# Values, convolution, u and head projections in blocks of 512 tokens instead of whole channel groups

## The reference, cut to what matters

```
xn   = x * rsqrt(mean(x*x) + 1e-6) * rms_w          # after a layernorm
V    = xn @ Wv.T + bv                                # 512 channels
vc   = causal depthwise convolution of V, 4 taps     # per channel, over the tokens
u    = silu(vc + conv_b)
dyn, seldt, selB, selC, beta, r_gate, u_gate = u @ (small matrices).T   # together 11 x 32 = 352 columns
...                                                  # coefficients of each head from these, 32 heads
scan over the tokens with k = K * sel_B, v = u * gate, read out with q = Q(u) * sel_C
...                                                  # group norm, gate, output projection, router, experts
```

## Time and profile before

| what | value |
|---|---|
| median of 3 runs | 1971.14 us (1969.77 to 1975.34) |
| the profiled execution's own time | 1970.1 us |
| its span | 1968.0 us |
| PE busy | 1347.6 us (68%) |
| DVE busy | 1436.4 us (73%) |
| ACT busy | 331.1 us (17%) |
| mean granted TensorE clock | 0.821 |

### The profile page before, as it was taken

The page is one execution under the profiler, slowest core; times in us unless marked ns, Lnnn a source line. Parts: engine busy times, 40 slices in busy tenths (PEclk is TensorE's granted clock), DMA queues, the critical chain, the costliest instruction groups (busy, mean ns, idle before and its releaser), DMA issues.

```text
span 1968.0 us, 12778 instructions
## 1 busy us (share of the span) xinstructions
PE 1347.6 (68%) x4176; PEld 753.7 (38%) x4176; DVE 1436.4 (73%) x2382; ACT 331.1 (17%) x592; POOL 0.2 (0%) x4
## 2 busy tenths in 40 slices
PE   2690276753088869356559999948388877399994
PEld 1250022212044445223335555535154445166662
DVE  3718799997899988856385999978999989500003
ACT  2312000001000002142332111122000011223331
POOL 0000000000000000000000000000000000000000
PEclk9895566665599989668879999969699989599997
DMA  3000010101011120210011222112111010122221
GB/s 123 0 0 0 11 43 32 43 11 64 0 32 43 43 85 11 86 49 0 0 32 57 94 72 88 54 64 86 43 43 53 22 43 0 48 66 82 75 78 43
DMA packets 49955, 89.66 MB, mean 46 GB/s; under 512 B 4450, under 2 KB 39650, under 8 KB 48867
## 3 DMA queue, kind: packets, MB, share of 16 engines
q1 hardware_dynamic: 49890, 88.87, 13.1%
HBM read 68.93 MB, written 19.92 MB: 45 GB/s over the span
## 4 chain that ended last, share of the span: by engine, by line
DVE 50%; PE 35%; issue 9%; ACT 4%; SPq 1%; DMA 1%; DVEq 0%; ACTq 0%
PE ps L513 9%; PE ps L525 9%; PE ps L389 5%; PE ps L364 4%; DVE work L1009 4%; DVE uT L719 3%; PE ps L390 3%; DVE small L988 3%; DVE work L989 2%; DVE small L724 2%; DVE work L1048 2%; DVE work L1035 2%; DVE kz L1018 2%; DVE work L959 2%; DVE work L719 2%
## 5 line engine op out<-in xcount | busy, mean ns | idle before, releaser
L440 PE MATMUL ps<-wshare,uT 128*128 128x512 f32 x512 | 251.0, 647 | 53.6 <-DVE kz L1018 53.6
L525 PE MATMUL ps<-kz 128*128 128x256 f32 x1024 | 243.5, 381 | 46.1 <-ACT kz L679 46.1
L389 PE MATMUL ps<-wshare,xnT 128*128 128x512 f32 x256 | 166.1, 783 | 142.4 <-DVE wshare L905 142.4
L513 PE MATMUL ps<-kz 128*128 128x512 f32 x512 | 246.7, 605 | 7.9 <-DMA kz<-in_w 7.2
L525 PEld LDWEIGHTS ps<-kz 128*128 128x128 f32 x1024 | 195.5, 191 | 127.2 <-issue 59.1
L440 PEld LDWEIGHTS ps<-wshare,uT 128*128 128x128 f32 x512 | 103.9, 209 | 181.0 <-issue 121.8
L1148 DVE TENSOR_TENSOR kz<-kz,b_s 128x256 f32<-128x256 f32 x32 | 13.6, 425 | 212.7 <-ACT kz L663 211.8
L679 ACT ACTIVATE kz<-ps,small 128x512 f32<-128x512 f32 x128 | 87.8, 687 | 396.2 <-PE ps L513 396.2
L389 PEld LDWEIGHTS ps<-wshare,xnT 128*128 128x128 f32 x256 | 55.4, 240 | 221.2 <-DVE wshare L905 146.3
L513 PEld LDWEIGHTS ps<-kz 128*128 128x128 f32 x512 | 97.7, 194 | 91.3 <-issue 84.4
L364 PE MATMUL ps<-wshare,uT 128*128 128x352 f32 x256 | 79.9, 476 | 37.5 <-ACT uT L598 37.5
(11 more groups left out here) (223 smaller groups left out, 1836.6 us busy)
## 6 DMA issues: line engine op xcount, KB each, us to landing
kz<-in_w SPq DMA_DIRECT2D x128, 256.0 KB, 3.0
kap_d<-kz SPq DMA_DIRECT2D x26, 512.0 KB, 2.8
kz<-kap_d SPq DMA_DIRECT2D x26, 512.0 KB, 3.3
uT<-in_x SPq DMA_DIRECT2D x2, 2048.0 KB, 8.0
wshare<-in_wq SPq DMA_DIRECT2D x2, 2048.0 KB, 7.9
coef<-in_x SPq DMA_DIRECT2D x2, 2048.0 KB, 7.8
wshare<-in_wk SPq DMA_DIRECT2D x2, 1024.0 KB, 12.1
x_d<-coef SPq DMA_DIRECT2D x1, 2048.0 KB, 6.2
```

The costliest lines, as they stand in the source:

```text
L389: mm(o, xnT[:, k, j * P:(j + 1) * P], wk_s[:, k, c, :], start=(k == 0), stop=False)
L440: t = mm(ps[:, 2 * (j % 2) + c, :], uT3[:, k, j * P:(j + 1) * P], wq_s[:, k, c, :], start=(k == 0), stop=(k == KI - 1))
L513: t = mm(ps[:, 4 + i % 2, :], w1_r[r][:, k, (f % 2) * P:(f % 2 + 1) * P], x2T[:, k, n * 512:(n + 1) * 512], start=(k == 0), stop=(k == KM ...
L525: t = mm(ps[:, 6 + q // 2, (q % 2) * DM:(q % 2 + 1) * DM], hbuf(i)[:, q * P:(q + 1) * P], w2_r[r][:, f % 2, :], start=(f == 0 and q % 2 == ...
```

## The change

It does five things:

- PE makes the values by blocks of tokens, in the order 3, 0, 1, 2, with the four groups inside a block.
- There are four `vbuf` buffers, one for each group: three in `work` and one in `kz`. The third reaches over the place of the rope table. ACT evicts all 16 units first, and then applies Silu to 16 pieces of 128 x 512, in the order of the blocks 0 to 3.
- DVE does the convolution by blocks. In a block it interleaves the four groups, so that each instruction waits for one four places earlier, and not for the one in front (`mark` and `after` in place of `link`). From block 1 on, it evicts the four head tiles of the block before, once a block is done.
- The head projections wait for u block by block, not for all of it. DVE no longer waits for each eviction to end before the next.
- The rope table is loaded after the convolution in both batches, since its place is in use until then. In batch 1 this stands behind the loads of the first four pairs of expert weights and before the others.

```diff
@@ -90,7 +90,9 @@
         w2_r = [kz[:, 9728 + 1024 * r:10240 + 1024 * r].rearrange("p (f n) -> p f n", f=2) for r in range(WR)]
         r_tok = kz[:, 13312:17408].rearrange("p (j d) -> p j d", j=L)
         VB = 19 * P
-        vbuf = [work[:, i * VB:(i + 1) * VB].rearrange("p (j c) -> p j c", c=P) for i in range(2)]
+        vbuf = [v.rearrange("p (j c) -> p j c", c=P) for v in
+                (work[:, 0:VB], work[:, VB:2 * VB], work[:, 2 * VB:3 * VB], kz[:, 0:VB])]
+        NORD = (3, 0, 1, 2)
         sall = coef[:].rearrange("p (q j h) -> p q j h", q=NSM, j=L)
         sall_j = coef[:].rearrange("p (q j h) -> p j q h", q=NSM, j=L)
         uT3 = uT[:].rearrange("p (g t) -> p g t", g=KI)
@@ -241,8 +243,7 @@
                 sp.dma_start(wk_s, wk.rearrange("(k p) i n -> p k i n", p=P)).then_inc(wk_loaded, 16)
 
             def load_rope(b):
-                if b > 0:
-                    sp.wait_ge(kq_used, b * 2 * L)
+                sp.wait_ge(conv_done, b * NV + NV)
                 sp.dma_start(HS(14), rope[:]).then_inc(rope_loaded, 16)
 
             def choose_experts(b):
@@ -281,16 +282,17 @@
             load(wo_s[:], wo.rearrange("(k p) n -> p k n", p=P))
             load(wr_s[:], wr.rearrange("(k p) n -> p k n", p=P))
             load(group[:], group_d[:])
-            load_rope(0)
             for b in range(B):
                 if b > 0:
                     load_wa(b)
-                    load_rope(b)
                     load_x(b)
                     sp.wait_ge(x1_ready, b * L)
                     sp.dma_start(x1_d[:], x1_tok).then_inc(x1_stored, 16)
                     chosen = choose_experts(b - 1)
-                    load_pairs(b - 1, chosen, 0, pairs_for(UNITS[0]))
+                    load_pairs(b - 1, chosen, 0, WR)
+                load_rope(b)
+                if b > 0:
+                    load_pairs(b - 1, chosen, WR, pairs_for(UNITS[0]))
 
                 for i in range(L):
                     if i < L - 3:
@@ -347,7 +349,7 @@
                 pe.wait_ge(wa_loaded, b * 32 + 32)
                 pe.wait_ge(xt_done, b * L + L)
                 for i in range(KI * NCH):
-                    g, n = i // NCH, i % NCH
+                    n, g = NORD[i // KI], i % KI
                     if i >= 4:
                         pe.wait_ge(v_done, b * NV + i - 3)
                     for k in range(KM):
@@ -356,8 +358,8 @@
                     t.then_inc(v_ready, 1)
 
             def head_projections(b):
-                pe.wait_ge(u_ready, b * KI + KI)
-                for j in range(L):
+                for j in range(L):
+                    pe.wait_ge(u_ready, b * NV + KI * (j // 4 + 1))
                     if j >= 2:
                         pe.wait_ge(sm_done, b * L + j - 1)
                     for k in range(KI):
@@ -583,19 +585,17 @@
                     t.then_inc(xt_done, 1)
 
             def values_and_u(b):
-                for g in range(KI + 1):
-                    if g < KI:
-                        if g >= 2:
-                            act.wait_ge(conv_done, b * KI + g - 1)
-                        for n in range(NCH):
-                            i = g * NCH + n
-                            act.wait_ge(v_ready, b * NV + i + 1)
-                            af(vbuf[g % 2][:, 3 + 4 * n:7 + 4 * n, :],
-                               ps[:, i % 4, :].rearrange("p (j c) -> p j c", c=P),
-                               ACT.Identity, bias=col[:, C_BV + g:C_BV + g + 1]).then_inc(v_done, 1)
-                    if g >= 1:
-                        act.wait_ge(conv_done, b * KI + g)
-                        af(uT3[:, g - 1, :], uT3[:, g - 1, :], ACT.Silu).then_inc(u_ready, 1)
+                for i in range(NV):
+                    n, g = NORD[i // KI], i % KI
+                    act.wait_ge(v_ready, b * NV + i + 1)
+                    af(vbuf[g][:, 3 + 4 * n:7 + 4 * n, :],
+                       ps[:, i % 4, :].rearrange("p (j c) -> p j c", c=P),
+                       ACT.Identity, bias=col[:, C_BV + g:C_BV + g + 1]).then_inc(v_done, 1)
+                for i in range(NV):
+                    n, g = i // KI, i % KI
+                    act.wait_ge(conv_done, b * NV + i + 1)
+                    ug = uT3[:, g, n * 512:(n + 1) * 512]
+                    af(ug, ug, ACT.Silu).then_inc(u_ready, 1)
 
             def heads(b):
 
@@ -720,6 +720,16 @@
 
             MUL, ADD, SUB, MAX = ALU.mult, ALU.add, ALU.subtract, ALU.max
 
+            def after(n):
+
+                dve.wait_ge(vec_chain, n)
+
+            def mark(ins):
+
+                n_chain[0] += 1
+                ins.then_inc(vec_chain, 1)
+                return n_chain[0]
+
             def stats(j, src):
                 link(v.bn_stats(st6[:, j, :], src))
                 link(v.bn_aggr(mv[:, j, :], st6[:, j, :]))
@@ -751,26 +761,48 @@
                     dve.wait_ge(xc_ready, b * L + j + 1)
 
             def convolution(b):
+
+                def coeff(g, k):
+                    return col[:, C_CW + 4 * g + k:C_CW + 4 * g + k + 1]
+
+                def acc(n, g):
+                    return uT3[:, g, n * 512:(n + 1) * 512].rearrange("p (j c) -> p j c", c=P)
+
                 for g in range(KI):
-                    dve.wait_ge(v_done, b * NV + (g + 1) * NCH)
-                    V, acc = vbuf[g % 2], uT3[:, g, :].rearrange("p (j c) -> p j c", c=P)
-                    link(v.memset(V[:, 0:3, 0:1], 0.0))
-                    link(v.tensor_copy(V[:, 0:3, 1:P], V[:, L:L + 3, 0:P - 1]))
-                    w = lambda k: col[:, C_CW + 4 * g + k:C_CW + 4 * g + k + 1]
-                    link(tsc(acc, V[:, 3:19, :], w(3), col[:, C_CB + g:C_CB + g + 1], MUL, ADD))
-                    for k in (2, 1):
-                        link(stt(acc, V[:, k:k + L, :], w(k), acc, MUL, ADD))
-                    stt(acc, V[:, 0:L, :], w(0), acc, MUL, ADD).then_inc(conv_done, 1)
-                    dve.wait_ge(conv_done, b * KI + g + 1)
-
-            def heads(b):
-                if b > 0:
+                    mark(v.memset(vbuf[g][:, 0:3, 0:1], 0.0))
+                dve.wait_ge(v_done, b * NV + KI)
+                for g in range(KI):
+                    seen = mark(v.tensor_copy(vbuf[g][:, 0:3, 1:P], vbuf[g][:, L:L + 3, 0:P - 1]))
+                after(seen)
+                for n in range(NCH):
+                    dve.wait_ge(v_done, b * NV + (min(n + 2, NCH)) * KI)
+                    for g in range(KI):
+                        seen = mark(tsc(acc(n, g), vbuf[g][:, 3 + 4 * n:7 + 4 * n, :], coeff(g, 3),
+                                        col[:, C_CB + g:C_CB + g + 1], MUL, ADD))
+                    for k in (2, 1, 0):
+                        for g in range(KI):
+                            after(seen - KI + 1 + g)
+                            o = stt(acc(n, g), vbuf[g][:, k + 4 * n:k + 4 * n + 4, :], coeff(g, k), acc(n, g), MUL, ADD)
+                            if k > 0:
+                                last = mark(o)
+                            else:
+                                o.then_inc(conv_done, 1)
+                        if k > 0:
+                            seen = last
+                    if n >= 1:
+                        head_tiles(b, n - 1)
+                head_tiles(b, NCH - 1)
+
+            def head_tiles(b, n):
+                if b > 0 and n == 0:
                     dve.wait_ge(x1_stored, 16 * b)
-                for j in range(L):
+                for j in range(4 * n, 4 * n + 4):
                     dve.wait_ge(sm_ready, b * L + j + 1)
                     tt(sall_j[:, j], ps[:, 6 + j % 2, 0:NSM * H].rearrange("p (q h) -> p q h", q=NSM),
                        bsm_s[:].rearrange("p (q h) -> p q h", q=NSM), ADD).then_inc(sm_done, 1)
-                    dve.wait_ge(sm_done, b * L + j + 1)
+
+            def heads(b):
+                dve.wait_ge(sm_done, b * L + L)
                 tt(HS(2), sall[:, 1], sall[:, 2], ADD).then_inc(hd_vec, 1)
                 dve.wait_ge(hd_vec, b * 5 + 1)
                 dve.wait_ge(rope_loaded, b * 16 + 16)
@@ -875,16 +907,6 @@
             def wide(ap):
 
                 return ap.unsqueeze(len(ap.shape)).to_broadcast([*ap.shape, HD])
-
-            def after(n):
-
-                dve.wait_ge(vec_chain, n)
-
-            def mark(ins):
-
-                n_chain[0] += 1
-                ins.then_inc(vec_chain, 1)
-                return n_chain[0]
 
             def pass_1(b):
                 X = tmp[:, 0:2048].rearrange("p (a i n) -> p a i n", a=2, i=2)
```

## The result

The changed kernel takes 1982.45 us (median of four runs, 1980.71 to 1983.32) against 1970.73 for the kernel before. The ratio is 1.0048, with a 95% interval of 1.0032 to 1.0065. So it is slower by about half a per cent, where no change was forecast as the likeliest, at 1974.5 us. The time lies within the stated range of 1962 to 1984, but outside the forecast's own of 1969 to 1980. The profiled execution took 1983.3 us, with a span of 1981.5.

A forecast was written before the change was run, and what follows sets the result against it. DVE, ACT and PE taking turns were taken to bound the stretch, 79.1 us per batch; 74.5 of order plus 6.3 for clock falls make 80.8, 3.4 us longer in all: 1974.5 us, range 1962 to 1984.

The forecast's parts named there:

- What bounds the stretch: From the convolution's first instruction to the coefficients (L774), DVE, ACT and PE take turns: 79.1 us per batch before the change.
- the order within it: Convolution blocks 2 and 3 alternate with head tiles, so overlap is partial: 74.5 us per batch at full clock.
- T: The first instruction of the convolution on DVE, from which the forecast counts times; expected to stay where it is.
- The block of the convolution: On DVE, one block of 4 tensor_scalar and 12 scalar_tensor_tensor takes 9.7 us, bounds 8.5 and 11.7.
- 20 of the 36.5 us: Convolution time per batch said to stand still one behind the other with 28.4 us of head tiles.
- the rival in which nothing overlaps: DVE instructions in convolution blocks 2 and 3 do not overlap: each block 2.0 us longer, 1982.5 us; chance 0.17.
- That the clock falls in each gap: PE's clock falls in three idle gaps per batch, 4.4 us before the first tile, about 6 before tiles 6 and 10.
- What a fall costs: Slow head tiles on PE after each clock fall: 2.1 us for each of three, 6.3 us per batch.
- That every stage behind L774 stays as it was: All stages from the start of the coefficients on keep their lengths, so the stretch's loss passes whole to the end, twice.
- the forecast's own sign: The forecast is wrong if L774 comes before T + 77 or after T + 84, or time moves behind L774.
- The rope table and the buffers: Later rope load on SP costs 0, bounds -0.5 and +0.5; the change of buffers costs nothing.
- The verdict: Whole kernel: 1974.5 us, no change within 0.3%; chances 0.59 the same, 0.29 slower, 0.12 faster.

The follow-up runs named there:

- fillers: Unused matmuls put into PE's three idle gaps of each batch of the changed kernel: 1963.2 us, ratio 0.9945 to the kernel before.
- second trace: The kernel before run once more with no edit, for another trace: 1972.6 us.
- early Silu: Changed kernel, but ACT applies Silu to the four pieces of block 0 between its last evictions: 1975.9 us, ratio 1.0012 to the kernel before.
- the version with both edits: Changed kernel with Silu of block 0 between the last evictions, and evictions of tiles 0 to 9 between convolution steps of blocks 1 to 3: 1938.2 us.

## Why the prediction was right or wrong

- **What bounds the stretch, and the order within it: right.** First tile at T + 24.1 (81.86 - 57.74), as forecast; the Silu behind the last eviction; DVE waiting in its list at the evictions; gaps of 4.28 and twice 6.18 us for the 4.4 and 6 forecast. Less what the tiles took beyond 2.37 us each, the stretch is 74.9 us in both batches, for 74.5; with the clock held up by fillers it was 75.7.
- **The block of the convolution: right.** From 94.58 to 104.36 it is 9.78 us, for 9.7. The 0.09 us by which the tensor_tensor pairs overlap hold for the scalar_tensor_tensor too, which last 0.75 us and start 0.66 apart. (The forecast's "20 of the 36.5 us" is 20 of 39 by its own sum; nothing hangs on it.) The waits back in place made four instructions 3.15 us instead of 2.65, so the rival in which nothing overlaps is refuted, though its total of 1982.5 us happens to be the one measured. The rule of the Trainium skill (VectorE: DVE Perf Modes, Rules for kernel authors) that the drain cannot be avoided by leaving out semaphores is contradicted here: 0.66 us apart without the wait on the neighbour, 0.79 with it.
- **That the clock falls in each gap: right. What a fall costs: too small.** This is the term that was mis-sized. The forecast took 2.1 us for each of three, from the two slow starts of the kernel before. Measured against 2.37 us a tile, the three stretches of tiles in batch 0 are 2.7, 3.1 and 2.3 us longer, 8.0 in all for 6.3; those of batch 1 come to 7.2. The stretch thus became 82.6 us in the mean for 80.8, which doubles the loss from 3.4 to 7 us. The fillers split this otherwise. With the clock up each stretch of tiles still took 0.25 us more than 2.37 a tile, so the clock's own part was 7.3 and 6.5 us, 0.6 above the forecast's 6.3 in the mean, and the other 1.2 us of the miss lie in the order, 75.7 for 74.5. In the second gap the clock fell late, a microsecond before the restart at 104.94, so that nearly all of the time at 0.50 fell on tiles:

```profile
103.00:105.00 2.00, 0.06 (x1) 0.09 (x1) 2.00 (x5) 1.90 (x4) 0.00 (x0) 0.71 0.00 0
105.00:107.00 2.00, 2.00 (x4) 1.25 (x5) 0.22 (x1) 0.02 (x1) 0.00 (x0) 0.50 0.00 0
```

- **That every stage behind L774 stays as it was: wrong.** This is the step that failed. The key pass of batch 0 was 3.8 us longer and its gates 2.7, and by the forecast's own sign, time that moves behind L774, this counts against it. The kernel before has long stages too in its own second trace (214.9 and 48.4), so they were there to be had before the change, but one trace could not show it. In the key pass the long length goes with a late first rise of the clock (see the last section). Why the changed kernel had the long ones in both traces and, by the narrow band of its nine runs, probably in most, is not shown.
- **The rope table and the buffers: nothing of them is seen.** From the coefficients to the key pass it is 88.8 us in batch 0 before and after, and 102.0 and 102.1 in batch 1, so nothing waited for the rope, and the first instructions of the convolution come as before.
- **The verdict.** The forecast put 0.59 on no change and 0.29 on slower. The direction of the sum (+3.4 us) and the alternation behind it were right, the likeliest verdict was not. The sum was short by 3.6 us in the stretch, and by what the key pass and the gates gave on top. That the time still lies in the stated range is in part luck: the range reaches beyond 1980 only for the rival in which nothing overlaps, and that one did not come true. Against the 14 later runs of the kernel before the loss is 8.0 us, of which the stretch explains 7.

## What to carry to other kernels

Splitting a stage in blocks lets two engines overlap only if neither has to stand in its own list for the other: work out where the evictions stand in the list of the engine that also produces the next block. Over both batches the same blocks with the evictions together cost 7 us of stretch, and with one eviction behind each four instructions they gained 24 (29 with the early Silu). A split also turns one long idle stretch of PE into several short ones, and each of them can cost a slow start of 2 to 3 us; cheap fillers showed what that is worth, 6.6 us per batch here.

## What was not expected of the hardware

- A stage with alternating PE and DVE has more than one length under one program: 210.3 and 214.9 us for the key pass in two traces of the kernel before. The length goes with the first rise of the clock in it. In the four traces with 214.1 to 214.9 us the clock first rose 27.5 to 28.0 us behind the first tile, in the nine with 207.6 to 211.5 it rose 5 to 12 us behind it. What sets the moment of that rise no run shows. First the changed kernel, then the kernel before:

```profile
229.60:257.40 27.80, 21.75 (x26) 6.90 (x26) 15.11 (x15) 0.00 (x0) 0.00 (x0) 0.50 0.09 38
```

```profile
226.40:237.30 10.90, 8.54 (x10) 2.86 (x10) 4.04 (x4) 0.00 (x0) 0.00 (x0) 0.50 0.12 48
237.50:240.70 3.20, 2.04 (x7) 0.71 (x6) 1.64 (x2) 0.00 (x0) 0.00 (x0) 1.00 0.00 0
```

- Unwaited neighbours on DVE overlap by 0.13 us against waited ones also where they read per-partition scalars (0.66 for 0.79 us at 128 x 512), and the 0.06 us that this form lasts longer than one without such a scalar is not hidden: tensor_tensor pairs are 0.60 us apart.
- In the version with both edits PE waited 2.00 us before its first tile in each batch. The six tiles behind took 16.16 us in batch 0, with a slow start, and 14.47 in batch 1, without one:

```profile
79.76 16.16 PE L366 MATMUL ps<-wshare,uT 128*128 128x352 f32 x48 [2.00 <-ACT uT L605]
...
885.95 14.47 PE L366 MATMUL ps<-wshare,uT 128*128 128x352 f32 x48 [2.00 <-ACT uT L605]
```
